# Seven weight transfers on ScalarE's queue issued behind the first stage's weight preparation

## The reference, cut to what matters

```python
x = x + conv(ln_c(x))     # relation-aware gates over space and over channels
t = tokens(x)
t = t + ffn(ln_t(t))      # 8 experts, router picks 2
```

## Time and profile before

| | us |
|---|---|
| median of 3 runs (lowest, highest) | 1772.88 (1771.52, 1775.07) |
| the profiled execution | 1769.24 |
| its span in the trace | 1767.4 |
| PE busy | 1681.3 (95%) |
| DVE busy | 1432.0 (81%) |
| ACT busy | 1180.4 (67%) |
| POOL busy | 1110.7 (63%) |

### The profile page before, as it was taken

One profiled execution on the slowest core, in us unless ns is written; L12 is line 12 of the kernel. 1 busy time (PEld: TensorE's weight loads), 2 busy tenths in 40 slices (PEclk: granted clock), 3 DMA queues, 4 the chain that ended last, 5 costly groups with the idle time before them and its releaser, 6 DMA issues.

```text
span 1767.4 us, 38965 instructions
## 1 busy us (share of the span) xinstructions
PE 1681.3 (95%) x13140; PEld 1281.1 (72%) x13140; DVE 1432.0 (81%) x4704; ACT 1180.4 (67%) x3346; POOL 1110.7 (63%) x1268
## 2 busy tenths in 40 slices
PE   4789999999999999999999999999999999999985
PEld 3567777777777777777777777777777777777673
DVE  4557888888888888888888888888888888888766
ACT  3557666667766767776676776666677667677543
POOL 1245666676666777666667666666766667675555
PEclk9899999999999999999999999999999999999998
DMA  5122222111222211222221122221112222111110
GB/s 140 37 75 74 76 90 93 71 69 66 93 74 93 93 56 68 81 93 74 93 87 53 65 92 76 91 93 68 72 66 93 74 93 92 56 66 65 56 56 37
DMA packets 56179, 135.15 MB, mean 76 GB/s; under 512 B 16268, under 2 KB 18333, under 8 KB 55982
## 3 DMA queue, kind: packets, MB, share of 16 engines
q1 hardware_dynamic: 55320, 130.81, 21.2%
q10 hardware_dynamic: 662, 1.84, 0.4%
HBM read 106.50 MB, written 26.13 MB: 75 GB/s over the span
## 4 chain that ended last, share of the span: by engine, by line
PE 73%; DVE 13%; ACT 8%; issue 2%; POOL 2%; DMA 1%; SPq 0%; ACTq 0%; POOLq 0%; DVEq 0%
PE low L1246 6%; PE rot L1111 5%; PE rot L1101 5%; PE rot L1102 5%; PE low L1248 5%; PE low L1247 5%; PE high L1246 5%; PE rot L1037 4%; PE high L1248 4%; PE high L1247 4%; ACT part L809 4%; PE rot L1200 3%; PE rot L971 3%; PE rot L981 2%; PE rot L1004 2%; ACT j L703 2%
## 5 line engine op out<-in xcount | busy, mean ns | idle before, releaser
L570 POOL TENSOR_TENSOR part<-part 128x256 f32<-128x256 f32 (+1 forms) x416 | 372.7, 896 | 378.4 <-DVE part L1693 376.1
L809 ACT ACTIVATE part<-low,gv 128x128 f32<-128x128 f32 (+1 forms) x1664 | 468.7, 372 | 149.4 <-PE low L1248 75.6
L1693 DVE SCALAR_TENSOR_TENSOR part<-high,gv,part 128x128 f32<-128x128 f32 x1536 | 421.3, 340 | 22.5 <-ACT part L809 11.5
L575 POOL TENSOR_TENSOR otok<-part 128x128 f32<-128x128 f32 (+1 forms) x416 | 224.9, 541 | 32.6
L1101 PE MATMUL rot<-x1h,wch 128*128 128x256 f32 x960 | 230.7, 281 | 0.0
L1102 PE MATMUL rot<-x1h,wcl 128*128 128x256 f32 x960 | 227.8, 278 | 0.0
L1246 PE MATMUL low<-weh,xh 128*128 128x512 f32 x384 | 174.3, 454 | 18.5 <-ACT part L809 10.9
L753 ACT ACTIVATE chan<-rot,bc 128x256 f32<-128x256 f32 x160 | 68.8, 471 | 172.3 <-PE rot L1113 172.2
L1101 PEld LDWEIGHTS rot<-x1h,wch 128*128 128x128 f32 x960 | 181.0, 189 | 3.2 <-issue 0.3
L1102 PEld LDWEIGHTS rot<-x1h,wcl 128*128 128x128 f32 x960 | 181.0, 189 | 2.6
L1246 PE MATMUL high<-weh,xh 128*128 128x512 f32 x384 | 169.3, 441 | 3.0 <-DVE part L1693 3.0
(11 more groups left out here) (246 smaller groups left out, 3893.3 us busy)
## 6 DMA issues: line engine op xcount, KB each, us to landing
xin<-in_x SPq DMA_DIRECT2D x32, 784.0 KB, 6.1
x<-in_x SPq DMA_DIRECT2D x32, 784.0 KB, 4.3
cen<-shift_rows SPq DMA_DIRECT2D x32, 784.0 KB, 4.1
out<-x SPq DMA_DIRECT2D x64, 392.0 KB, 2.4
y_ch<-rstd_rows SPq DMA_DIRECT2D x32, 768.0 KB, 3.8
otok<-in_ggs_w SPq DMA_DIRECT2D x1, 600.2 KB
tok<-in_ggs_w SPq DMA_DIRECT2D x1, 600.2 KB
rstd_rows<-both_rows SPq DMA_DIRECT2D x32, 7.0 KB
```

The lines of the kernel that those rows point to most:

```text
L570: nc.gpsimd.tensor_tensor(part[0:n, slot, 0:2, :], part[0:n, slot, 0:2, :], part[0:n, slot, 2:4, :], ALU.add).then_inc(sem("half_sum"), 1)
L575: nc.gpsimd.tensor_tensor(otok[0:n, t, :], part[0:n, slot, 0, :], part[0:n, slot, 1, :], ALU.add).then_inc(sem("token_ready"), 1)
L809: last = nc.scalar.activation(part[0:n, turn % RING, e, :], src, ACT.Copy, scale=gv[par(p, back)][0:n, t, e:e + 1])
L1693: last = nc.vector.scalar_tensor_tensor(out=own, in0=src, scalar=gv[par(p, back)][0:n, t, HALF + e:HALF + e + 1], in1=own, op0=ALU.mult, o ...
```

## The change

In ACT's program the call of `wide_issue`, which issues the seven `big` transfers, is taken out of the ahead step, where it stood between the four token copies and `rstd_copy`, and is put behind `space_weights()`, in front of the first of the pipeline's steps. The transfers, their order, their semaphore and all waits stay as they are.

```diff
@@ -814,7 +814,6 @@
                     x_tokens(0, 1, 1)
                     x_tokens(1, 0, 1)
                     x_tokens(1, 1, 1)
-                    wide_issue()
                     rstd_copy(1)
                     return
 
@@ -890,6 +889,7 @@
 
             step(act, 0, 1, ahead=True)
             space_weights()
+            wide_issue()
             steps(act, step)
```

## The result

The changed kernel takes 1777.41 us in the median of 14 runs (1773.22 to 1780.28), the kernel before 1772.25 us in 14 runs beside it (1768.69 to 1775.79). The ratio is 1.0031, with a 95% interval of 1.0023 to 1.0040: 5.5 us slower, 4.1 to 7.1. The profiled execution has a span of 1771.7 us, 4.3 us over that of the kernel before.

What follows compares the result with a forecast made beforehand. The prediction took the startup chain to DVE's `wide_loaded` wait, then PE, as bounding. The 8.6 us gain was spent by transfers starting 15.4 us later: release +2.8 us, 1772.88 to 1775.7 us, range 1770.5 to 1780.0.

Steps and rivals of the forecast that it cites:

- the chain: Startup: row's write, SP's 21 wide issues and last landing lead to DVE's `wide_loaded` wait, ending at 35.67 us.
- The reading that four engines carry 77 rows each: Startup, q10: 68- and 76-row pieces lie on four engines, 77 rows each with the others, 10.2 us.
- The gains of 8.6 and 6.5 us: Startup: small list lands at 15.0 instead of 23.58; SP goes on 6.5 us earlier after the row's write.
- the duration of q10: ACT's queue carrying the seven moved transfers: forecast 12.6 us, from 25.2 to 37.8.
- The bounds, 10.2 and 16.5: Limits on q10's duration in us: the 77 rows alone, or the earlier 13.05 plus both big SP loads.
- the 0.45 that I had granted for less `ggs` traffic: q10 forecast at 12.6 us, near the earlier 13.05, with the rest of the `ggs` weights out of the way.
- My argument that SP's loads queue behind the small packets: During q10: SP's two big loads hardly weigh on the four engines, queuing behind some 105 small packets per engine.
- the rival of the crossing loads: During q10: SP's load rows alternate with q10's on four engines; release 42.4, +6.7 us, 1779.6 us; chance 0.20.
- The release: End of DVE's wait for `wide_loaded`: forecast to move from 35.67 to 38.5, +2.8 us.
- The clock: PE's granted clock around its first burst: longer idling could shift half-clock stretches; 1.7 us allowed either way, nothing taken.
- The early release: Rival at the wide wait: tail due to traffic, transfers at 385 GB/s, release near 30.5, 1767.7 us; chance 0.08.

Runs made afterwards that it cites:

- the run with the wait: Changed kernel, with SP waiting for all wide weights before loading unit 1's input and the expert weights; ratio to the kernel before 1.0017.
- group G: Probe added behind the last store of the kernel before: two 128-row loads on SP's queue beside two 68-row loads on ACT's; ended after 7.9 us.
- The second execution: Profiled execution of the changed kernel run once more, unaltered, beside the kernel before; span 1774.6 us, ratio 1.0031.
- group F: Probe added behind the last store of the kernel before: four 68-row loads at once to partitions 0-67; 84 GB/s, 10.2 us.
- the split alone: Changed kernel, with the 68- and 76-row pieces issued as 64 rows and the rest, without SP's added wait; ratio to the kernel before 1.0004.
- either new place: Seven transfers moved, unsplit, behind `space_weights()` (changed kernel, ratio 1.0031) or behind the copy of the first unit's row (ratio 1.0000), both against the kernel before.

## Why the prediction was right or wrong

**Right as to the chain and what the change frees.** The reading that four engines carry 77 rows each, one by one with SP's small packets, gave 15.0 for the small list (14.98), 1.4 us for the row's write (1.51), 24.2 for the first issue (24.11), 29.8 for the end of ACT's `gx` (29.84) and 27.7 for the load of unit 1 (28.44). The gains of 8.6 and 6.5 us at these places were all there and were all spent, because the large transfers became the last to arrive.

**The step that failed is the duration of q10**, 12.6 us against 16.0. The bounds, 10.2 and 16.5, held it. Of the 3.4 us, 2.3 are SP's loads, as the run with the wait shows. The other 1.1 (13.7 against 12.6) are the 0.45 that I had granted for less `ggs` traffic, which aren't there, and 0.6 beyond the 13.05 measured before, whose cause stays open. My argument that SP's loads queue behind the small packets on the four engines was right as far as it went: the release comes 0.7 us behind q10's last row, and the input's own rows on these engines come later still. By the trace's packet records 192 of its 256 rows, which is 16 for each of twelve engines, run by 35.2 us, none up to 40, and the last 64 behind that. My argument left out that the rows on the four engines are slowed while the loads run on the other twelve, from 34 to 21 packets a microsecond. So the rival of the crossing loads, which I gave 0.20, is the one that came by its own sign, a q10 of over 14 us, and its release of 42.4 lies nearer to 41.79 than the forecast's 38.5. It was half true in the mechanism: right in the cause, with 2.3 us in place of 3.5, and wrong in the place, since they don't alternate on the four engines. How the twelve slow the four isn't shown; in the probe of both kinds (group G) they hardly did.

**The release**, 38.5 forecast, came at 41.79: +6.1 us in place of +2.8. **The clock** added what I had left at nothing. PE's first transposes behind the wait take 1.12 us for four, where they took 0.66, and from the release to ACT's copies of unit 1's tokens (L657) it is 12.1 us in place of 11.1, in both executions of the changed kernel. That makes the 7.07 us of the row writes. The second execution has half the clock on record from before the release to 47 us (columns as in the earlier trace rows), where the kernel before had it from 37.5 to 40.9 only:

```profile
28.00:47.00 19.00, 4.67 (x16) 2.30 (x17) 4.92 (x14) 4.52 (x11) 0.00 (x0) 0.50 0.58 144
```

I had allowed 1.7 us either way.

**The time.** 1775.7 was forecast against a median of 1772.88, 1777.41 was measured against 1772.25, within the range of 1770.5 to 1780.0. I had 0.59 on a change within 0.2% and 0.33 on slower by more. It was slower by 0.31%: the direction was right, the size half of what came. That the range held it is owed to the rival of the crossing loads, which it was drawn to take in, and not to the forecast's own mechanism. That the shift reaches the end in full holds for the changed kernel: 7.07 us stay constant through the steady state. My reason for it, that PE has hardly a gap from the first steps on, was too strong. Before the change PE is busy for 132.8 us of the 150 from 30 to 180, and in four of the runs above the shift changed by 1.8 to 4.2 us there.

**The early release**, 0.08, is out: a tail that is due to traffic would have vanished with the wait, and q10 stayed at 13.7 us; loads of 68 rows with nothing beside them ran at 84 GB/s (group F). The full rate of 385 GB/s on which it rested was not reached by the probes' loads to 64 or fewer partitions of one side (188 to 207 GB/s over the stretch).

## What to carry to other kernels

Before moving a transfer, divide its rows by the engines it really runs on, and ask which partitions it writes: here 68 rows ran on four of 16 engines, and 64 rows, written to one half of the partitions, took twice the time a row. The transfer that is freed isn't the one that ends the wait: the gains of 8.6 and 6.5 us at the small list and at the row were real and worth nothing, since the moved transfers themselves had a spare 12 us and lost 18. Mending the transfer (64 rows and the rest, 2 to 4 us) was worth more than either new place for it, 5.5 us lost and nothing gained.

## What the runs showed of the hardware that was not expected

- On the four engines two queues take turns by single records: 68 small ones and 68 of q10 from 38 to 40 us, as 69 and 69 in the earlier trace rows. In the trace's packet records nearly every row of 3136 bytes on the four has a small one just ahead of it.
- Loads that write 64 partitions of one side take 0.24 us a row with all 16 engines busy, against 0.124 us for 128 partitions: 201 to 207 GB/s against 300 over the stretch.
- The issue of a transfer can hold its engine's queue for long while its earlier ones are outstanding: 3.27 and 7.50 us for two issues on SP, with the wide weights still on their way. In the run in which SP waits first, the same two take 0.47 and 0.43 us. With the split alone they take 0.49 and 4.61. What the issue waits for isn't shown.
- PE ran its first transposes behind 16 us of idleness at the pace of half the clock (1.12 us for four) while the profile of the first execution has the granted clock at 1.00 from 42 to 43 us. The second execution has the same 1.12 us with 0.50 on record from 28 to 47 us, and in the kernel before four at 39.89 took 1.12 us with 0.50 on record. So the 1.00 is likely a gap in the first execution's record; that isn't shown.
